# First attention of a fused two-layer kernel: scores in two row groups of TensorE, and fewer, larger transfers around them

## The reference

```python
x = x + _L0_xattn_ref(_layernorm(x, axis=-1), ctx_2048, ctx_2048)

def _L0_xattn_ref(q, k, v):             # q: normed x, k = v: context
    # 8 heads of 16 of the 128 rows; each head's columns (256) are its tokens
    qn = _l2norm(qh, axis=-2)
    kn = _l2norm(kh, axis=-2)
    qk = ALPHA * jnp.einsum('bhdq,bhdk->bhqk', qn, kn)
    sm = jax.nn.softmax(qk, axis=-1)
    out = jnp.einsum('bhqk,bhdk->bhdq', sm, vh)
```

## Time and profile before

| what | value |
|---|---|
| time, median of 3 runs | 799.24 us (798.59 to 799.4) |
| the profiled execution: its own time | 800.01 us |
| the profiled execution: span from first to last instruction | 798.3 us |
| mean granted clock of PE | 0.961 |
| busy share of the span: PE, DVE, ACT, POOL | 85%, 83%, 78%, 67% |
| DMA transfers of queue q1 | 98.70 MB, 61.7% of 16 engines |

### The profile page before, as it was taken

How to read it: one execution, slowest core, us unless ns; L and a number is a source line. 1 busy time by engine, 2 the same in 40 slices (tenths; PEclk the granted TensorE clock), 3 DMA queues, 4 the chain that set the end, 5 groups by cost and what they waited for, 6 DMA issues and landing times. The chain is left out here.

```text
span 798.3 us, 17290 instructions
## 1 busy us (share of the span) xinstructions
PE 677.3 (85%) x5139; PEld 423.0 (53%) x5139; DVE 661.1 (83%) x1576; ACT 624.3 (78%) x2122; POOL 534.5 (67%) x764
## 2 busy tenths in 40 slices
PE   0075799999578678999999999999999999978995
PEld 0043255455234345666666666666666666645552
DVE  6756556764689769999999999999999999978994
ACT  0556477777399769999999999999999999968661
POOL 1413756663357888888788878887887888753673
PEclk9997599999799989999999999999999999999997
DMA  8502555542024356897887798788879787865244
GB/s 278 199 1 54 138 155 148 142 129 86 11 67 106 64 106 126 147 144 129 148 139 142 127 154 139 134 138 154 139 135 144 143 136 133 153 113 93 58 125 122
DMA packets 323795, 99.80 MB, mean 125 GB/s; under 512 B 294868, under 2 KB 322934, under 8 KB 323446
## 3 DMA queue, kind: packets, MB, share of 16 engines
q1 hardware_dynamic: 323702, 98.70, 61.7%
HBM read 20.01 MB, written 6.29 MB: 33 GB/s over the span
## 5 line engine op out<-in xcount | busy, mean ns | idle before, releaser
L1235 ACT ACTIVATE psum<-psum,arena 128x256 f32<-128x256 f32 x256 | 135.9, 531 | 21.1 <-DVE arena L1355 21.0
L1311 DVE SCALAR_TENSOR_TENSOR arena<-psum,arena 128x256 f16<-128x256 f32 x256 | 110.9, 474 | 1.1 <-ACT arena L1252 1.1
L1252 ACT ACTIVATE arena<-psum,arena 128x256 f16<-128x256 f32 x256 | 100.3, 474 | 7.4 <-issue 3.4
L1444 PE MATMUL psum<-arena 128*128 128x512 f16 x384 | 94.2, 381 | 8.1 <-DVE arena L1338 7.9
L1189 POOL TENSOR_TENSOR arena<-arena 128x512 f32<-128x512 f32 x64 | 81.1, 1267 | 27.8 <-DVE arena L1330 27.8
L1406 PE MATMUL psum<-wq_t,arena 128*128 128x512 f16 x384 | 94.5, 383 | 5.5 <-ACT arena L1266 2.8
L1431 PE MATMUL psum<-arena 128*128 128x256 f16 x768 | 95.6, 275 | 1.0 <-DMA arena<-arena 0.8
L1459 PE MATMUL psum<-wo_t,arena 128*128 128x256 f16 x768 | 95.0, 274 | 0.1
L305 ACT ACTIVATE arena<-psum 128x1024 f32<-128x1024 f32 x64 | 63.1, 1019 | 33.2 <-PE psum L391 33.2
L1459 PEld LDWEIGHTS psum<-wo_t,arena 128*128 128x128 f16 x768 | 75.5, 98 | 23.2 <-issue 1.1
L1220 POOL TENSOR_TENSOR arena<-arena 128x512 f16<-128x512 f32 x64 | 74.1, 1157 | 20.0 <-DVE arena L1355 19.9
(11 more groups left out here) (187 smaller groups left out, 1612.5 us busy)
## 6 DMA issues: line engine op xcount, KB each, us to landing
arena<-split_scratch SPq DMA_DIRECT2D x96, 64.0 KB, 2.6
arena<-arena SPq DMA_TRANSPOSE x272, 3.3
split_scratch<-arena SPq DMA_DIRECT2D x32, 128.0 KB, 2.1
arena<-in_L_ffn_w SPq DMA_DIRECT2D x2, 1024.0 KB, 6.8
x_rows<-in_L_xattn_Wq SPq DMA_DIRECT2D x1, 2048.0 KB, 14.4
ctx_t<-in_L_xattn_Wo SPq DMA_DIRECT2D x1, 2048.0 KB, 12.4
x_rows<-in_x SPq DMA_DIRECT2D x16, 128.0 KB, 2.3
arena<-in_ctx SPq DMA_DIRECT2D x16, 128.0 KB, 2.5
```

The lines of the kernel that those rows point to most:

```text
L1235: last = eng.activation(s_banks(u)[:, h, :], s_banks(u)[:, h, :], ACT.Exp, bias=bias[:, u % 2, h:h + 1], scale=r_q(u)[:, h:h + 1], accum_o ...
L1252: hi = eng.activation(p_hl[:, u % 2, 0, h, :], s_banks(u)[:, h, :], ACT.Copy, scale=share[:, u % 2, h:h + 1])
L1311: last = eng.scalar_tensor_tensor(p_hl[:, u % 2, 1, h, :], s_banks(u)[:, h, :], share[:, u % 2, h:h + 1], p_hl[:, u % 2, 0, h, :], ALU.mul ...
L1444: mm = eng.matmul(A_BANK, v[:, u % V_SLOTS, x, k, :], p_t[:, u % 2, w, :, k, :], start=(n == 0), stop=(n == 5))
```

## The change

- Scores: heads 0 to 3 stand on partitions 0 to 47 of `q_stack` and `k_stack`, heads 4 to 7 on partitions 64 to 111. A unit takes one head of each, and its four products alternate between the two row groups.
- Gather: each of its six transfers is made as two, one for each row group, so twelve of 32 KB for a batch.
- Rows of x: four transfers (1, 3, 6 and 6 batches) instead of one for a batch, issued with the loads of batches 0 to 3.
- Context: turned for two batches at once, 1024 columns wide instead of 512; its buffer holds four batches instead of two.
- Store: one transfer of 256 KB for a batch instead of two, issued by ACT at the end of its step instead of by SP.

```diff
-    ctx_hl = c.local("ctxhl_a", [P, 2, 2, D], F16)
-    q_stack = c.local("q_stack", [STACK, 2, HEADS, D], F16)
-    k_stack = c.local("k_stack", [STACK, 2, HEADS, D], F16)
+    ctx_hl = c.local("ctxhl_a", [P, 4, 2, D], F16)
+    q_stack = c.local("q_stack", [64 + STACK, 2, HEADS // 2, D], F16)
+    k_stack = c.local("k_stack", [64 + STACK, 2, HEADS // 2, D], F16)
...
+    ROW_GROUPS = (slice(0, 1), slice(1, 4), slice(4, 10), slice(10, 16))
...
-        return (0, 4, 1, 5)[m], (2, 6, 3, 7)[m]
+        return (0, 2, 1, 3)[m], (4, 6, 5, 7)[m]
...
-                eng.dma_start(c.x_rows[:, b, :], x_in[b, :, :]).then_inc(loaded[n], 16)
+                if b < len(ROW_GROUPS):
+                    group = ROW_GROUPS[b]
+                    eng.dma_start(c.x_rows[:, group, :], x_in[group, :, :].rearrange("b p n -> p b n"))\
+                       .then_inc(rows_loaded[b], 16)
                 eng.dma_start(yc[:, n, 1, :], ctx_in[b, :, :]).then_inc(loaded[n], 16)
             b = batch(s, CTX_TURN)
-            if b is not None:
+            if b is not None and b % 2:
+                n = b // 2 % 2
                 eng.wait_ge(S["ctx_low"], b + 1)
...
-                    eng.dma_start(q_stack[HD * k:HD * k + HD, p, :, :], src[part, :, :, 0:D])\
-                       .then_inc(stacked[p], 16)
+                    for j in range(2):
+                        eng.dma_start(q_stack[64 * j + HD * k:64 * j + HD * k + HD, p, :, :],
+                                      src[part, :, 4 * j:4 * j + 4, 0:D]).then_inc(stacked[p], 16)
...
-            b = batch(s, STORE)
-            if b is not None:
-                p = b % 2
-
-                eng.wait_ge(S["low"], b + 1)
-                wait(eng, stacked[p], 96 * (b // 2))
-                for part in range(2):
-                    eng.dma_start(split_dram[p, part], halves[:, p, part, :]).then_inc(stored[p], 16)
...
@@ ScalarE, at the end of its step
+            b = batch(s, STORE)
+            if b is not None:
+                p = b % 2
+
+                eng.wait_ge(S["low"], b + 1)
+                wait(eng, stacked[p], 192 * (b // 2))
+                eng.dma_start(split_dram[p].rearrange("s p n -> p s n"), halves[:, p, :, :]).then_inc(stored[p], 16)
...
-                for j, h in enumerate(heads_of(v)):
-                    for k in range(2):
-                        mm = eng.matmul(score_banks(v % 2)[:, j, D * k:D * k + D], k_stack[:, vp, h, P * k:P * k + P],
-                                        q_stack[:, vp, h, :], start=True, stop=True)
+                for k in range(2):
+                    for j, h in enumerate(heads_of(v)):
+                        half = slice(64 * j, 64 * j + STACK)
+                        mm = eng.matmul(score_banks(v % 2)[:, j, D * k:D * k + D],
+                                        k_stack[half, vp, h % 4, P * k:P * k + P],
+                                        q_stack[half, vp, h % 4, :], start=True, stop=True)
```

More of the change, by code:

```diff
@@ L188, in part_a @@
     loaded = [c.sem(f"a_loaded{n}") for n in range(4)]
+    ROW_GROUPS = (slice(0, 1), slice(1, 4), slice(4, 10), slice(10, 16))
+    rows_loaded = [c.sem(f"a_rows_loaded{n}") for n in range(len(ROW_GROUPS))]
     stacked = [c.sem(f"a_stacked{n}") for n in range(2)]
@@ L225, in sync @@
                 wait(eng, S["ctx_low"], b - 3)
-                eng.dma_start(c.x_rows[:, b, :], x_in[b, :, :]).then_inc(loaded[n], 16)
+                if b < len(ROW_GROUPS):
+                    group = ROW_GROUPS[b]
+                    eng.dma_start(c.x_rows[:, group, :], x_in[group, :, :].rearrange("b p n -> p b n"))\
+                       .then_inc(rows_loaded[b], 16)
                 eng.dma_start(yc[:, n, 1, :], ctx_in[b, :, :]).then_inc(loaded[n], 16)
             b = batch(s, CTX_TURN)
-            if b is not None:
+            if b is not None and b % 2:
+                n = b // 2 % 2
                 eng.wait_ge(S["ctx_low"], b + 1)
-                eng.dma_start_transpose(c.ctx_t[:, b, :, :].rearrange("p s (k r) -> p (s k) r", k=2),
-                                        ctx_hl[:, b % 2, :, :].rearrange("p s n -> p (s n)"))\
-                   .then_inc(ctx_turned[b % 2], 16)
+                eng.dma_start_transpose(c.ctx_t[:, b - 1:b + 1, :, :].rearrange("p b s (k r) -> p (b s k) r", k=2),
+                                        ctx_hl[:, 2 * n:2 * n + 2, :, :].rearrange("p b s n -> p (b s n)"))\
+                   .then_inc(ctx_turned[n], 16)
             b = batch(s, GATHER)
@@ L236, in sync @@
                 p = b % 2
-                eng.wait_ge(stored[p], 32 * (b // 2 + 1))
+                eng.wait_ge(stored[p], 16 * (b // 2 + 1))
                 wait(eng, S["scores"], PAIRS * (b - 1))
@@ L241, in sync @@
                 for k, part in enumerate((0, 1, 0)):
-                    eng.dma_start(q_stack[HD * k:HD * k + HD, p, :, :], src[part, :, :, 0:D])\
-                       .then_inc(stacked[p], 16)
+                    for j in range(2):
+                        eng.dma_start(q_stack[64 * j + HD * k:64 * j + HD * k + HD, p, :, :],
+                                      src[part, :, 4 * j:4 * j + 4, 0:D]).then_inc(stacked[p], 16)
                 for k, part in enumerate((0, 0, 1)):
-                    eng.dma_start(k_stack[HD * k:HD * k + HD, p, :, :], src[part, :, :, D:2 * D])\
-                       .then_inc(stacked[p], 16)
-            b = batch(s, STORE)
-            if b is not None:
-                p = b % 2
-                eng.wait_ge(S["low"], b + 1)
-                wait(eng, stacked[p], 96 * (b // 2))
-                for part in range(2):
-                    eng.dma_start(split_dram[p, part], halves[:, p, part, :]).then_inc(stored[p], 16)
+                    for j in range(2):
+                        eng.dma_start(k_stack[64 * j + HD * k:64 * j + HD * k + HD, p, :, :],
+                                      src[part, :, 4 * j:4 * j + 4, D:2 * D]).then_inc(stacked[p], 16)
             yield
         for p in range(2):
-            eng.wait_ge(ctx_turned[p], 16 * (BATCHES // 2))
+            eng.wait_ge(ctx_turned[p], 16 * (BATCHES // 4))
     def pool(eng):
@@ L267, in pool @@
             if b is not None:
[L268 to L271, removed]
+                n = b % 4
+                eng.wait_ge(loaded[n], 16 * (b // 4 + 1))
+                wait(eng, ctx_turned[n // 2], 16 * (b // 4))
+                eng.tensor_copy(ctx_hl[:, n, 0, :], yc[:, n, 1, :]).then_inc(S["ctx_high"], 1)
                 eng.wait_ge(S["ctx_high"], b + 1)
-                eng.tensor_tensor(ctx_hl[:, p, 1, :], yc[:, n, 1, :], ctx_hl[:, p, 0, :], ALU.subtract)\
+                eng.tensor_tensor(ctx_hl[:, n, 1, :], yc[:, n, 1, :], ctx_hl[:, n, 0, :], ALU.subtract)\
                    .then_inc(S["ctx_low"], 1)
@@ L285, in pool @@
                 eng.wait_ge(S["unit"], b + 1)
-                wait(eng, stored[p], 32 * (b // 2))
+                wait(eng, stored[p], 16 * (b // 2))
                 eng.tensor_copy(halves[:, p, 0, :], unit_rows[:, p, :]).then_inc(S["high"], 1)
@@ L363, in vector @@
                 p, n = b % 2, b % 4
-                eng.wait_ge(loaded[n], 32 * (b // 4 + 1))
+                eng.wait_ge(next(sem for rows, sem in zip(ROW_GROUPS, rows_loaded) if b < rows.stop), 16)
                 eng.bn_stats(stats[:, p, :], c.x_rows[:, b, :]).then_inc(S["var"], 1)
@@ L386, in tensor @@
                 if v % PAIRS == 0:
-                    eng.wait_ge(stacked[vp], 96 * (b // 2 + 1))
+                    eng.wait_ge(stacked[vp], 192 * (b // 2 + 1))
                 wait(eng, S["exps"], v - 1)
-                for j, h in enumerate(heads_of(v)):
-                    for k in range(2):
-                        mm = eng.matmul(score_banks(v % 2)[:, j, D * k:D * k + D], k_stack[:, vp, h, P * k:P * k + P],
-                                        q_stack[:, vp, h, :], start=True, stop=True)
+                for k in range(2):
[4 more added lines that the diff above has]
+                                        q_stack[half, vp, h % 4, :], start=True, stop=True)
                 mm.then_inc(S["scores"], 1)
@@ L419, in tensor @@
                         for g in range(4):
-                            q, j = v % PAIRS - 1 + g // 2, g % 2
+                            q, j = v % PAIRS - 1 + g % 2, g // 2
                             h = 2 * g + odd
```

## The result

| what | before | after |
|---|---|---|
| median time, each run beside the other on one chip | 799.12 us (20 executions, 797.3 to 800.26) | 800.99 us (20 executions, 798.35 to 803.45) |
| the profiled execution: own time, span | 800.01, 798.3 us | 801.44, 799.7 us |

The ratio is 1.0025, with a 95% interval of 1.0017 to 1.0032: slower by 2.0 us (1.4 to 2.6). The forecast was slower by 4.0, so the direction came out and the size is half. Ratios are taken over the executions of the usual, fast state alone; one execution of `before_held` (3816 us) stands far apart and is left out of them.

A forecast was written before the change was run, and what follows sets the result against it. Bound before: a two-batch loop through PE, DVE and POOL (7.42 us a batch), SP's queue close behind. SP's net +17.5 us makes SP the bound; the stage ends 4.0 us later: 803.2 us, range 795 to 811.

The forecast's parts named there:

- SP's queue is the bound: First attention: SP's issues, occupied 115.3 us between first and last gather instead of 97.8, set the pace; chance 0.55.
- the sum: First gather at 85.4 plus 115.3 us of SP; batch 15's scores at 203.0; stage 4.0 us later; median 803.2.
- what pays for them: Savings on SP's queue against +44.2 us for gathers: row loads -6.2, stores -13.5, turns -6.9.
- the scores: PE's eight scores a batch: 0.6 us instead of 1.04 if the two row groups run side by side.
- the store on ACT: ACT's store lands after about 2.4 us; rival that it closes a loop: about 812 us, chance 0.10.
- POOL's square: PE's wait for it ahead of every second length sum, 0.76 us before, would be gone or rare.
- what could make it wrong: Signs against: half gather issues under 0.43 us, PE's clock falls in new gaps, SP still waits several us for POOL.
- the last term of the sum: Behind the first attention: everything moves with the stage's end by 4.0 us, 800.01 to 804.0, or 803.2 for the median.
- Should a half gather cost half: Faster rival, SP's queue: SP needs some 77 us, the loop sets the pace, 6.3 us gained, 793; chance 0.22.

The follow-up runs named there:

- before_held: Kernel before plus 22 idle products in PE's two waits at the second attention's start; 797.97 us, 0.9980 of before.
- groups_alone: Kernel before with only the two row groups and twelve gathers added; 833.38 us, 1.0433 of before.
- rest_alone: Kernel after with six gathers and one row group, keeping larger row loads, paired turns and ACT's store; 798.13 us, 0.9994 of before.
- before_late4: Kernel before plus 38 unread score products (about 4.2 us) ahead of the first attention's last value products; 805.1 us, 1.0055 of before.
- after_again: Kernel after run a second time, nothing changed; 1.0030 of before.
- after_third: Kernel after run a third time, nothing changed; 1.0040 of before.
- merged: Kernel after with two gathers a batch instead of twelve, the store laying three row copies side by side in three transfers; 798.36 us, 0.9982 of before.
- experiment 5: 22 idle products in PE's two waits at the second attention's start, in both kernels: before 797.97 us (0.9980), after 799.9 us (1.0013).

## Why the prediction held in its mechanism, and where its size failed

*Right: SP's queue is the bound.* The steps of the sum up to the stage's end came out. A half gather costs 0.469 with the step to the next (0.46 taken, 0.473 the upper bound). SP is occupied for 116.3 us (115.3). The first gather starts at 84.33 (85.4), and batch 15's scores at 203.47 (203.0). PE leaves the stage 4.2 us later in the first pair of profiles (4.0). SP's waits are gone, and PE waits for gathers. Part of the closeness is luck: the first gather came 1.1 sooner than summed, SP needed 1.0 more, and the clock took about half a microsecond at the end. `groups_alone` confirms the terms apart: +34.6 us for the gathers without what pays for them, with SP's occupied time within 0.1 us of the sum.

*Right with a small miss: the scores.* 0.61 us for eight (0.6 taken).

*Right: the store on ACT.* It lands in 2.3 us (2.4 taken), and `rest_alone` shows no cost of it together with the row loads and the turns.

*Half right: POOL's square.* The wait was to be gone or rare. It came five times, 5.9 us in all, up to 1.5; as I read the timeline, because with shorter scores PE reaches the length sum sooner. SP worked through without a break all the same, so it cost nothing by itself, but the prediction named the clock only as what could make it wrong, and the clock did fall, twice (granted 0.66 from 112 to 117 us, 0.79 from 195 to 201). The rest of this paragraph is read from the timelines and not tested by a run. The first fall, behind a wait of 1.49 for the square, was made good in PE's later waits for gathers. The second came behind the wait of 2.14 for a gather at 197.09, and batch 15's scores began straight behind the slowed groups at 203.47, when the last gather, issued by 201.24 and 1.9 us in landing, had been there for some tenths: a cost of about half a microsecond.

*Wrong: the last term of the sum.* The step that failed is "PE leaves the stage 4.0 us later, and all that follows moves with it: 800.01 + 4.0 = 804.0". It carries the 4.0 at its whole size from one profiled execution to the median, where the change was measured at 2.0, 2.4 and 3.2 us; with the draw at the second attention's start held down at 2.6; and the stage cut off and timed at 2.9. All lie between half and four fifths of 4.0. In the three pairs of profiles the stage did end later, by 4.2, 3.6 and 5.5 us, 4.4 in the mean; but what follows did not keep the distance: its length changed by -2.8, -2.5 and +0.1, -1.7 in the mean. A pure delay does move on whole (`before_late4`). What the sum put at nothing is that the stretch behind the stage can run at either clock: the execution that it starts from had the low clock at the twelve products, so its rest was 592.4, and without that it is about 590.

*A wrong figure in a rival.* Should a half gather cost half, SP would need some 72 us (97.8 - 6.2 - 13.5 - 6.9 + 1.1) and not 77. The 793 of that case does not hang on it, since the loop sets the pace either way.

*Open.* How the missing 1 to 2 us divide between a stage that on average costs less than its profiled executions show, and draws behind it that are kinder to the kernel after, isn't settled, and so the cause of the smaller size stays open. The profiles speak for the draws, the timed runs with the later parts cut off or with the draw held (2.9 and 2.6) for the stage. The times of one kernel alone spread over 3 to 5 us. Nor does one place explain all: in `after_again` and `after_third` the clock fell near there as well, at other groups (0.84 from 281 to 292 us in both), with rests of 589.5 and 589.9 all the same. What is shown is the first pair: there 2.5 of the 2.8 us given back are those three groups.

## What to carry to other kernels

A queue that issues transfers is an engine like the others: add up its issues before you split them, since a transfer of 32 KB cost SP no less than one of 192 KB (0.469 us with the step to the next; `merged` issues two in 0.79). A gain on PE of 0.43 us for each eight scores, beside a loop that goes through other engines too, does not pay for six more issues a batch. Change the layout at the store, so that few large transfers read it back; and where a faster group opens a regular wait on PE, look at the granted clock behind it before the gain is counted. A sum that starts from one profiled execution carries the luck of that execution: where a stretch behind the change can run at either clock, take it from several profiles.

## What the runs showed of the hardware that was not expected

- Waits of PE of 1.30 to 1.49 us, once in 14.3 us, were enough to bring the clock down to its lower level now and then (`merged`: behind two of five). With 0.8 us of useless products in each the profile showed 1.00, and with the 22 products of experiment 5 the ratio moved from 0.9982 to 0.9913.
- The clock fell with PE never idle, too: in `before_late4` PE was busy without a gap from 205.5 to 214.2 us, and its granted clock was 1.00 up to 208 and 0.50 from 209.5 on, during the 38 score products on 48 rows and behind them.
- The clock's fall is not the same from one execution to the next of the same kernel: the twelve products at the second attention's start took 2.77 us in two profiles of before and 1.47 in the third.
- A 32 KB gather landed in 1.9 us, a 64 KB one in 2.6, one of 192 KB in 3.3 (`merged`, over 48 partitions): for these gathers landing grows with the size, and issuing does not.
